# Two constant tiles of the causal mask product stored in bf16 instead of float32r

## The chip, the cores and the metric

One NeuronCore of one Trainium2 chip runs the whole program. The metric is the device time in microseconds (us). The kernel before takes 2742.83 us, the median of three runs (2741.75 to 2742.94).

## The reference

A decoder of two layers works on x, 4 batches of 512 rows with 256 features, and on a context of 4 x 1024 rows with 192 features. What is computed, in order:

```
x = LN(x + attn_L0(x))            # causal self-attention, 16 heads of 16
x = LN(x + xattn_L0(x, ctx))      # cross-attention, 1024 keys
x = LN(x + soft_moe_L0(x))        # 8 experts, 128 slots each
x = LN(x + attn_L1(x))            # causal self-attention
x = LN(x + xattn_L1(x, ctx))      # cross-attention
x = LN(x + block_L1(x))           # causal self-attention, then top-2 of 8 experts
```

In each causal layer the scores of query q against key k are `q.k/4`, with every k > q masked out, and then a softmax over k and the product with the values:

```
w = einsum('bhnd,bhmd->bhnm', q, k) / 4
w = where(tril, w, NEG); w = softmax(w); attn = einsum('bhnm,bhmd->bhnd', w, v)
```

## The kernel before, in words

There are three causal layers: a0 and a1, and a2 (the attention inside the last block). There are two cross layers, c0 and c1. `stage_attentions` runs twice: "first" does a0 and c0, "second" does a1, c1 and a2. Its work is cut into groups of four heads of one batch: 16 groups a layer, numbered n. `attention_plan` writes one list of events by hand (`body(n)`), and each engine walks it in order and does its own part. No planner with costs reorders it, apart from pieces of projections and norms that are spread in between by rough weights.

Heads have 16 features. Queries and keys are each split into two parts whose sum is the float32 value, so that one product with a contraction of 64 rows serves one head. Two heads (h = 0 and 1) lie in partitions 0 to 63 and 64 to 127, and are issued as a pair of products on the two halves of TensorE's rows; a second pair of heads is p = 0 or 1. These tiles are float32r (float32 read in one pass).

In a group, each head's scores are computed twice, in two layouts:

- `unit` (L1413): queries on partitions, keys along the columns. VectorE adds the mask and takes the row maximum (L1729 in causal layers; L1733 in cross layers, without a mask). A `chain` of small VectorE steps (L1757 to L1770) makes minus the maxima in bf16 parts, and TensorE turns them (L1467, `shift`, bf16) and ScalarE copies them out as `shift_T` (L1646, float32r).
- `scores`, event (t, p): the keys of key tile t (128 of them) on partitions, the queries from 128 t on along the columns: 512, 384, 256 and 128 columns for t = 0 to 3. Three kinds of product are added up in one PSUM bank for each h: the scores (L1426), in causal layers the mask (L1432), and the row maxima (L1436). ScalarE then takes the exponential (L1635).

`values` (L1448) multiplies the probabilities with the values, four heads side by side in 32 columns each (float32, 128 rows). All banks but one are shared by a ring of 7.

The code of a `scores` event on TensorE, from L1424 on:

```
for h in range(2):
    pe.matmul(bank_of(event, h)[:, q0:SEQ], keys_of(n)[own, p, ...], qs[r][own, p, q0:SEQ], start=True, stop=False)
if layer.causal:
    for x in range(2):
        for h in range(2):
            pe.matmul(bank_of(event, h)[:, q0:q0 + 64 * (x + 1)], c.pick[own, x, :],
                      c.mask_kq[own, x, 0:64 * (x + 1)], start=False, stop=False)
for h in range(2):
    filled(pe.matmul(bank_of(event, h)[:, q0:SEQ], c.choose[own, p, :], shift_T[n % 2][own, q0:SEQ], ...), event)
```

`pick` (the weights) holds two halves of an identity: half x picks rows 64 x to 64 x + 63 of the mask. `mask_kq` (the moving side) holds 0 or -1e30 for those 64 keys, and is used for 64 columns (x = 0) and 128 columns (x = 1). Each of the four mask products loads its own 128 columns of weights. There are 3 layers x 16 groups x 4 tiles x 2 = 384 causal `scores` events, and so 1536 mask products and as many weight loads.

Both tiles are made once, in `stage_constants`: GpSimd makes `ident_bf` and `tri_kq` in bf16, and VectorE copies them into `pick` and `mask_kq` (8 copies, L159).

Of the kernel before, what the change touches and what calls it, by code (L numbers as in the profile page):

```python
# [23 lines left out]
F32R = mybir.dt.float32r  # L24
BF16 = mybir.dt.bfloat16
# [5 lines left out]
P = 128  # L31
# [72 lines left out]
@staged  # L104
def stage_constants(c):

    nc = c.nc
    c.x_tok = c.keep("x_tok", [P, NT, D])  # L110
    c.ident = c.keep("ident", [P, P])
    c.ident_bf = c.keep("ident_bf", [P, P], BF16)
    c.pick = c.keep("pick", [P, 2, P], F32R)
    c.choose = c.keep("choose", [P, 2, P], F32R)
    c.mask_qk = c.keep("mask_qk", [P, SEQ])
    c.mask_kq = c.keep("mask_kq", [P, 2, P], F32R)
    c.eps = c.keep("eps", [P, 1])
    c.x_in = [c.ctx.enter_context(nc.semaphore(f"x_in{b}")) for b in range(BATCH)]
    c.made = c.ctx.enter_context(nc.semaphore("const_made"))
    filled = c.sem("const_filled")  # L120
    with (nc.sbuf_tensor("tri_kq", [P, P], BF16) as tri_kq,
          nc.sbuf_tensor("chosen", [P, 2, P], BF16) as chosen, nc.Block() as block):
        @block.sync
        def _(sp):
            for b in range(BATCH):
                sp.dma_start(c.x_tok[:, b * QT:(b + 1) * QT, :], c.args["x"][b].rearrange("(q p) d -> p q d", p=P)
                             ).then_inc(c.x_in[b], 16)

        @block.gpsimd
        def _(pool):  # L130
            for t in (c.ident, c.ident_bf, c.mask_qk, tri_kq):
                pool.memset(t[:, :], 0.0).then_inc(filled, 1)
            pool.memset(chosen[:, :, :], 0.0).then_inc(filled, 1)
            pool.memset(c.eps[:, :], LN_EPS).then_inc(c.made, 1)
            pool.wait_ge(filled, 5)
            for t in (c.ident, c.ident_bf):
                pool.affine_select(out=t[:, :], in_=t[:, :], compare_op=ALU.not_equal, fill=1.0, base=0,
                                   pattern=[[-1, P]], channel_multiplier=1).then_inc(c.made, 1)
            pool.affine_select(out=c.mask_qk[:, SEQ - P:SEQ], in_=c.mask_qk[:, SEQ - P:SEQ], compare_op=ALU.is_ge, fill=NEG_BIG,
                               base=0, pattern=[[-1, P]], channel_multiplier=1).then_inc(c.made, 1)  # L140
            pool.affine_select(out=tri_kq[:, :], in_=tri_kq[:, :], compare_op=ALU.is_ge, fill=NEG_BIG,
                               base=0, pattern=[[1, P]], channel_multiplier=-1).then_inc(c.made, 1)


            for i in range(6):
                if i:
                    pool.wait_ge(filled, 5 + 2 * i)
                for p in range(2):
                    pool.affine_select(out=chosen[:, p, :], in_=chosen[:, p, :], compare_op=ALU.not_equal, fill=1.0,
                                       base=-(64 * (i // 3) + 32 * p + i % 3), pattern=[[0, P]], channel_multiplier=1  # L150
                                       ).then_inc(filled, 1)

        @block.vector
        def _(v):
            v.wait_ge(c.made, 5)
            for dst, src in ((c.pick, c.ident_bf), (c.mask_kq, tri_kq)):
                for own in (slice(0, 64), slice(64, P)):
                    for x in range(2):
                        v.tensor_copy(dst[own, x, :], src[64 * x:64 * x + 64, :]).then_inc(c.made, 1)  # L159
            v.wait_ge(filled, 17)  # L160
            v.tensor_copy(c.choose[:, :, :], chosen[:, :, :]).then_inc(c.made, 1)
            v.wait_ge(c.made, CONSTANTS)
# [2359 lines left out]
def build(nc, args, out):  # L2522
    with ExitStack() as ctx:
        c = Core(nc, ctx, args, out)
        a = args
        stage_constants(c)

        def drams(name, keys):
# [170 lines left out]
```

## Time and profile before

| | us |
|---|---|
| median of three runs | 2742.83 |
| the profiled execution, own time | 2762.94 |
| its span, first to last instruction | 2761.2 |
| TensorE products busy in the span | 2504.2 (91%) |
| TensorE weight loads busy | 1439.7 (52%) |
| VectorE busy | 1496.9 (54%) |
| ScalarE busy | 1315.6 (48%) |

PE is TensorE's products and PEld its weight loads, which may overlap products. A busy time counts the latency of an instruction too, so that products in a pipeline overlap: their starts, not their lengths, show the pace. The mean granted clock of TensorE is 0.952 of full speed. The causal mask products run from 63 to 352 us (a0), 1345 to 1631 us (a1) and 2073 to 2332 us (a2); pieces of the layer after, and of the experts' gate in a2, lie among them.

### The profile page before, as it was taken

How to read it: one execution, taken by the hardware profiler on the slowest of the kernel's cores; microseconds unless marked ns; L12 is line 12 of the kernel's file. 1: busy time of each engine (PE TensorE's matmuls, PEld its weight loads, DVE VectorE, ACT ScalarE, POOL GpSimd, SP SyncE). 2: the span in 40 equal slices, each digit the busy share in tenths (PEclk: the TensorE clock that was granted, in tenths of full speed). 3: DMA queues.
4: the chain of work that ended last, by engine and by line, in shares of the span. 5: the costliest groups of instructions: out<-in, count | busy, mean ns of one | idle time of the engine just before them, and what ended most of it. 6: DMA issues, size and time to landing. Idle time of an engine off the chain costs nothing. (4 is left out here: it accounts for less than half of the span.)

```text
span 2761.2 us, 47077 instructions
## 1 busy us (share of the span) xinstructions
PE 2504.2 (91%) x15751; PEld 1439.7 (52%) x15752; DVE 1496.9 (54%) x4204; ACT 1315.6 (48%) x2826; POOL 455.4 (16%) x735
## 2 busy tenths in 40 slices
PE   5999999999979889999699999999998988599991
PEld 3555544444434456676365654444445555366761
DVE  2555777789744600013455598878756664322224
ACT  2655466677754521212255557766675543122220
POOL 4233212101100000000113322022122122110004
PEclk8999999999999999999799999999999987799995
DMA  7544534232800022203755443342322554121003
GB/s 222 160 142 142 144 100 107 54 85 58 267 1 1 1 98 67 95 12 115 201 151 142 140 115 85 81 107 62 109 77 81 165 165 148 52 63 34 31 31 97
DMA packets 156894, 276.76 MB, mean 100 GB/s; under 512 B 22928, under 2 KB 98960, under 8 KB 152208
## 3 DMA queue, kind: packets, MB, share of 16 engines
q1 hardware_dynamic: 152896, 262.56, 33.2%
q0 software_dynamic: 3792, 11.54, 1.3%
q8 instruction: 119, 1.95, 0.3%
q14 instruction: 87, 0.71, 0.1%
HBM read 195.51 MB, written 95.29 MB: 105 GB/s over the span
## 5 line engine op out<-in xcount | busy, mean ns | idle before, releaser
L1635 ACT ACTIVATE second_p<-psum 128x512 f32<-128x512 f32 (+3 forms) x1024 | 460.2, 524 | 248.7 <-PE psum L1436 233.4
L1635 ACT ACTIVATE first_p<-psum 128x512 f32<-128x512 f32 (+3 forms) x768 | 364.9, 551 | 150.1 <-PE psum L1436 146.8
L1733 DVE TENSOR_REDUCE second_max_parts<-psum 128x1 f32<-128x512 f32 x512 | 324.9, 685 | 54.6 <-PE psum L1413 44.5
L1733 DVE TENSOR_REDUCE first_max_parts<-psum 128x1 f32<-128x512 f32 x512 | 324.9, 685 | 52.0 <-PE psum L1413 42.7
L1729 DVE CUSTOM_DVE_ANT_0 second_masked<-psum,mask_qk 128x384 f32<-128x384 f32 (+3 forms) x512 | 229.7, 489 | 185.7 <-PE psum L1413 159.5
L1448 PE MATMUL psum<-second_p,second_v_aug 128*32 128x512 f32 (+3 forms) x2048 | 237.1, 535 | 0.5 <-ACT second_o_sum L1642 0.4
L1413 PE MATMUL psum<-second_k,second_q 64*128 64x512 f32 (+3 forms) x1024 | 211.9, 413 | 24.3 <-DMA second_k<-a_k_parts 11.4
L1426 PE MATMUL psum<-second_q,second_k 64*128 64x512 f32 (+3 forms) x1024 | 215.1, 416 | 5.8 <-DVE second_max_parts L1729 4.5
L1436 PE MATMUL psum<-second_shift_T,choose 64*128 64x512 f32 (+3 forms) x1024 | 198.3, 382 | 0.0
L1448 PE MATMUL psum<-first_p,first_v_aug 128*32 128x512 f32 (+3 forms) x1536 | 185.9, 556 | 1.2 <-ACT first_p L1635 0.7
L2512 ACT ACTIVATE routed_space<-psum,routed_bias 128x128 f32<-128x128 f32 x312 | 84.7, 382 | 213.3 <-PE psum L2437 213.3
L1729 DVE CUSTOM_DVE_ANT_0 first_masked<-psum,mask_qk 128x128 f32<-128x128 f32 (+3 forms) x256 | 114.5, 488 | 131.1 <-PE psum L1413 117.4
L1413 PEld LDWEIGHTS psum<-second_k,second_q 64*128 64x128 f32 x1024 | 101.2, 192 | 150.9 <-DVE second_max_parts L1733 87.1
L1413 PE MATMUL psum<-first_k,first_q 64*128 64x512 f32 (+3 forms) x768 | 166.0, 435 | 12.6 <-DMA first_k<-a_k_parts 6.6
L1426 PE MATMUL psum<-first_q,first_k 64*128 64x512 f32 (+3 forms) x768 | 163.0, 421 | 4.3 <-DVE first_max_parts L1733 3.4
L1426 PEld LDWEIGHTS psum<-second_q,second_k 64*128 64x128 f32 x1024 | 98.5, 188 | 113.0 <-issue 53.7
L1436 PE MATMUL psum<-first_shift_T,choose 64*128 64x512 f32 (+3 forms) x768 | 149.2, 384 | 0.0
L1413 PEld LDWEIGHTS psum<-first_k,first_q 64*128 64x128 f32 x768 | 74.1, 191 | 132.6 <-DVE first_max_parts L1733 85.5
L2427 PE MATMUL psum<-routed_up,routed_rows_T 128*128 x312 | 142.0, 598 | 0.9 <-issue 0.9
L2446 PE MATMUL psum<-routed_down,routed_space 128*128 x624 | 141.0, 379 | 0.0
L2134 DVE TENSOR_TENSOR soft_slots_T<-psum,soft_experts_down_bias 128x256 f32 (+1 forms) x32 | 13.6, 425 | 231.6 <-PE psum L2110 231.6
L1432 PEld LDWEIGHTS psum<-mask_kq,pick 64*128 64x128 f32 x1536 | 136.3, 193 | 4.6
(341 smaller groups left out, 3865.4 us busy)
## 6 DMA issues: line engine op xcount, KB each, us to landing
first_k<-c_k_parts SPq DMA_DIRECT2D x64, 256.0 KB, 4.7
second_q<-a_q_parts SPq DMA_DIRECT2D x128, 128.0 KB, 3.0
second_k<-a_k_parts SPq DMA_DIRECT2D x128, 128.0 KB, 3.0
second_k<-c_k_parts SPq DMA_DIRECT2D x64, 256.0 KB, 4.7
first_q<-a_q_parts SPq DMA_DIRECT2D x64, 128.0 KB, 3.2
first_k<-a_k_parts SPq DMA_DIRECT2D x64, 128.0 KB, 3.2
c_k_parts<-first_held SPq DMA_DIRECT2D x16, 512.0 KB, 3.1
first_q<-c_q_parts SPq DMA_DIRECT2D x64, 128.0 KB, 4.2
```

The lines of the kernel that those rows point to most:

```text
L1413: ins = pe.matmul(bank_of(event, h)[:, 0:width], qs[r][own, p, qt * P:(qt + 1) * P], keys_of(n)[own, p, k0:k0 + width], start=True, stop=True)
L1426: pe.matmul(bank_of(event, h)[:, q0:SEQ], keys_of(n)[own, p, t * P:(t + 1) * P], qs[r][own, p, q0:SEQ], start=True, stop=False)
L1432: pe.matmul(bank_of(event, h)[:, q0:q0 + 64 * (x + 1)], c.pick[own, x, :], c.mask_kq[own, x, 0:64 * (x + 1)], start=False, stop=False)
L1436: filled(pe.matmul(bank_of(event, h)[:, q0:SEQ], c.choose[own, p, :], shift_T[n % 2][own, q0:SEQ], start=False, stop=True), event)
L1448: ins = pe.matmul(c.psum[32 * j:32 * j + 32, PV_BANK, q0:SEQ], v_aug[n % 2][:, t, j, :], probs[at % 2][:, j, q0:SEQ], start=t == 0, stop=t ...
L1635: evacuated(act.activation(probs[tile % 2][:, 2 * h + p, q0:SEQ], bank[:, q0:SEQ], ACT.Exp, scale=scale), event)
L1729: evacuated(v.tensor_tensor_reduce(masked[:, done % 2, 0:width], bank[:, 0:width], c.mask_qk[:, SEQ - width:SEQ], 1.0, LEAST, ALU.add, ALU ...
L1733: evacuated(v.reduce_max(max_parts[n % 2][:, h, p, qt, k0 // BANK:k0 // BANK + 1], bank[:, 0:width], axis=AX_X), event)
L2134: v.tensor_tensor(eo[:, bass.ds(e, 1), t, :], c.psum[:, 4 + t, 0:D].unsqueeze(1), down_bias[r][:, :].unsqueeze(1), ALU.add).then_inc(s_rea ...
L2427: ins = pe.matmul(c.psum[:, UP_BANK + h, :], rows_T[r][:, k, :], up[:, bass.ds(e, 1), k, h * BANK:(h + 1) * BANK].rearrange("p o n -> p (o ...
L2446: ins = pe.matmul(c.psum[:, DOWN_BANK + r, 0:D], hidden[r][:, m, :], down[:, bass.ds(e, 1), m, :].rearrange("p o n -> p (o n)"), start=m = ...
L2512: act.activation(hidden[r][:, m, :], c.psum[:, TURN_BANK + m // PER, m % PER * P:(m % PER + 1) * P], ACT.Gelu, bias=bias[:, bass.ds(e * HM ...
```

## The change

Two tiles change their type, and nothing else in the program does. The products at L1432 then have bf16 on both sides. The products before and after them in the same bank (L1426, L1436) keep float32r. The copies at L159 become bf16 to bf16. The two tiles take 512 bytes of a partition each in place of 1024. The event lists are as before, in causal and in cross layers.

```diff
-    c.pick = c.keep("pick", [P, 2, P], F32R)
+    c.pick = c.keep("pick", [P, 2, P], BF16)
     c.choose = c.keep("choose", [P, 2, P], F32R)
     c.mask_qk = c.keep("mask_qk", [P, SEQ])
-    c.mask_kq = c.keep("mask_kq", [P, 2, P], F32R)
+    c.mask_kq = c.keep("mask_kq", [P, 2, P], BF16)
```

## Rows read from the trace of the kernel before

**Rows 1.** Busy time by engine in the three causal stretches.
```profile
core 0: us, PE busy (x) PEld busy (x) DVE busy (x) ACT busy (x) POOL busy (x), PEclk, DMA share, GB/s
63.00:352.00 289.00, 281.21 (x2278) 166.93 (x2276) 172.38 (x663) 159.87 (x369) 82.55 (x119) 0.98 0.52 147
1345.00:1631.00 286.00, 273.67 (x2248) 165.27 (x2244) 171.01 (x663) 154.48 (x358) 72.78 (x108) 0.97 0.54 147
2073.00:2332.00 259.00, 233.12 (x2088) 147.82 (x2084) 160.22 (x722) 125.58 (x312) 53.45 (x108) 0.89 0.42 129
```

**Rows 2.** Waits in 63 to 352 us: who waited for whom, total, times, longest.
```profile
DVE first_masked L1729 <- PE psum L1413: 76.9, 93, 2.6
ACT first_p L1635 <- PE psum L1436: 59.0, 58, 2.9
...
PEld psum L1426 <- DVE first_max_parts L1729: 13.5, 22, 0.8
```

**Rows 3.** The same in 2073 to 2332 us.
```profile
ACT second_p L1635 <- PE psum L1436: 92.4, 62, 4.6
...
PEld psum L1426 <- ACT second_p L1635: 13.2, 17, 1.8
...
PEld psum L1490 <- ACT second_oT L1650: 6.7, 2, 5.6
...
PEld psum L1426 <- DVE second_max_parts L1729: 5.9, 14, 0.8
```

**Rows 4.** Timeline, products then loads: a narrow event (t = 3) after a shift.
```profile
305.13 0.40 PE L1467 MATMUL psum<-ident_bf,first_shift 128*128 128x128 bf16 x4
305.46 0.33 PE L1426 MATMUL psum<-first_q,first_k 64*128 64x128 f32 x2
305.62 0.39 PE L1432 MATMUL psum<-mask_kq,pick 64*128 64x64 f32 x4
305.84 0.28 PE L1436 MATMUL psum<-first_shift_T,choose 64*128 64x128 f32 x2
305.95 0.45 PE L1413 MATMUL psum<-first_k,first_q 64*128 64x512 f32 x2
...
305.13 0.23 PEld L1467 LDWEIGHTS psum<-ident_bf,first_shift 128*128 128x128 bf16 x4 [0.41 <-issue]
305.45 0.19 PEld L1426 LDWEIGHTS psum<-first_q,first_k 64*128 64x128 f32 x2
305.56 0.30 PEld L1432 LDWEIGHTS psum<-mask_kq,pick 64*128 64x128 f32 x4
305.78 0.19 PEld L1436 LDWEIGHTS psum<-first_shift_T,choose 64*128 64x128 f32 x2
305.90 0.19 PEld L1413 LDWEIGHTS psum<-first_k,first_q 64*128 64x128 f32 x2
```

**Rows 5.** The same of a wide event (t = 0).
```profile
308.07 0.50 PE L1426 MATMUL psum<-first_q,first_k 64*128 64x512 f32 x2
308.42 0.33 PE L1432 MATMUL psum<-mask_kq,pick 64*128 64x64 f32 x4
308.59 0.45 PE L1436 MATMUL psum<-first_shift_T,choose 64*128 64x512 f32 x2
```

**Rows 6.** Loads of one form by line: busy us, mean ns of one.
```profile
L1432 PEld LDWEIGHTS psum<-mask_kq,pick 64*128 64x128 f32 x1536 | 136.3, 193 | 4.6
L1467 PEld LDWEIGHTS psum<-ident_bf,first_shift 128*128 128x128 bf16 x128 | 7.5, 99 | 14.9 <-issue 12.4 <-DVE first_shift L1770 2.6
```

**Rows 7.** Timeline of the loads: two bf16 loads before short products.
```profile
2215.35 0.10 PEld L1559 LDWEIGHTS psum<-second_both,second_tri 128*128 128x128 bf16 x1 [0.24 <-issue]
2215.36 0.10 PEld L1560 LDWEIGHTS psum<-second_earlier,second_ones 128*128 128x128 bf16 x1
```

**Rows 8.** Timeline of products: a change of tile shape, float32 on both sides.
```profile
237.70 0.22 PE L1413 MATMUL psum<-first_k,first_q 64*128 64x128 f32 x2
237.85 0.43 PE L1448 MATMUL psum<-first_p,first_v_aug 128*32 128x128 f32 x8
```

**Rows 9.** Timeline of the start: making the constants.
```profile
3.25 4.08 POOL L149 TENSOR_SCALAR_AFFINE_SELECT chosen<-chosen 128x128 bf16<-128x128 bf16 x12
3.32 1.05 DVE L159 CAST pick<-ident_bf 64x128 fp32r<-64x128 bf16 x4 [3.20 <-POOL tri_kq L141]
4.41 0.98 DVE L159 CAST mask_kq<-tri_kq 64x128 fp32r<-64x128 bf16 x4
7.37 0.29 DVE L161 CAST choose<-chosen 128x256 fp32r<-128x256 bf16 x1 [1.98 <-POOL chosen L149]
```

## The prediction

> **What bounds the kernel now.** I read the busy times of the three causal stretches first, since only they hold the changed products. In a0 the products are busy for 281 of 289 us and in a1 for 274 of 286, while VectorE and ScalarE stand at 54 to 60% [rows 1]. Busy time counts latency, so this alone does not prove that TensorE sets the pace. The waits do: in a0 VectorE waits 76.9 us for the products at L1413 and ScalarE 59.0 us for those at L1436, and the largest single wait of TensorE for another engine is 13.5 us [rows 2]. The other two engines are fed by TensorE. In a2 the balance is softer: 233 of 259 us, and TensorE waits 13.2 us for exponentials, 6.7 for a copy of outputs and 5.9 for maxima [rows 1, 3]. So time taken out of TensorE's stream counts nearly in full in a0 and a1, and less in a2.
>
> Then the timeline inside one `scores` event, to see whether products or weight loads set TensorE's pace. In the narrow event the loads start at 305.45, 305.56, (the second mask pair, inside the merged row of four), 305.78 and 305.90 [rows 4]: four steps over 0.45 us, 0.11 us for each pair of loads. The products between them have 128, 64, 128 and 128 columns. Had the columns set the pace, the pair with 64 would be followed twice as soon as those with 128; the step is the same for all. So here the loads are the limit, one pair each 0.11 us. A wide event shows the same behind its long first product: from the first mask product to the first of L1436 it is 308.59 - 308.42 = 0.17 us [rows 5]. I take a column at 0.42 ns, that is 2.4 GHz: the granted clock is 0.98 here, the upper of the two levels [rows 1]. The two mask pairs have 64 + 128 columns, 0.08 us; the rest is loading.
>
> **The loads.** The change halves nothing in the columns; what it can change is the load. A float32r load takes 193 ns in the mean, a bf16 load of the same 128 columns 99 ns [rows 6]. What counts is how soon the next may start. At L1559 and L1560 two bf16 loads start 0.01 us apart (2215.35 and 2215.36), before products of 32 columns [rows 7]; the four of L1467 fit in 0.23 us, three steps that hold (0.23 - 0.10)/3 = 0.04 us each with products of 128 columns between them [rows 4]. So a bf16 load holds the load path for 0.01 to 0.04 us where a float32r one holds it for 0.11. Both rows are loads of 128 rows; none in the trace has 64 rows in bf16, nor two halves side by side. I take 0.015, as the steps of L1467 are filled by products of 128 columns (0.053 us) anyway.
>
> The Trainium skill, page "TensorE: Matmul & The Clock Gate", section "LDWEIGHTS (loading the stationary operand)", puts a load at columns / 1.2 ns, 107 ns for 128, whatever the rows: the trace's step of 0.11 us agrees. The section "Weight-path perf modes" of the same page gives a faster load to 128 weights that are not FP32, four times in theory and about two times measured. By two times a bf16 load would hold the path for 54 ns and not for 15; that is my second case below.
>
> **The sum.** *Wide and middle events* (t = 0, 1, 2; 512, 384, 256 columns in the first product). The loads of the first mask pair lie behind the first product's columns and cost nothing now. The second mask pair's load must wait until the first mask pair has begun, and the load of L1436 until the second pair has: 0.11 us for the second. After the change the first mask pair's 64 columns (0.027 us) cover the 0.015 us of load. Gain 0.107 - 0.027 = 0.08 us. *Narrow events* (t = 3). Now it is 305.78 - 305.45 = 0.33 us from the first load to that of L1436 [rows 4]. After: the first load 0.107, its product's 128 columns 0.053, then the 64 columns 0.027 and the start of the second pair, in all 0.19. Gain 0.14 us. There are 96 events of each t: 96 x (3 x 0.08 + 0.14) = 36.5 us of TensorE's stream, 12.2 a layer.
>
> *What of it reaches the end.* Each place where TensorE waits for an engine that was not itself waiting for TensorE eats what was gained before it. Summing what TensorE's rows show against other engines, as in [rows 2, 3], I estimate 8% of a0's stretch, 11% of a1's and 19% of a2's in such waits, and their neighbourhood more: 0.85 of the gain in a0 and a1, 0.7 in a2. That is 12.2 x (0.85 + 0.85 + 0.7) = 29 us. What is late next is VectorE's masked maximum at L1729, and in a2 the exponential and the gate's chain.
>
> *The rest of the change.* The copies at L159 end near 5.4 us, and TensorE's start waits for `choose` at 7.37, which waits for GpSimd's 12 selects [rows 9]: faster or slower copies cost nothing up to 2 us. The moving side in bf16 gives nothing in columns, and its price cannot be less than the 0.027 us above. Half a kilobyte less of each tile only moves addresses: nothing.
>
> The profiled execution took 2762.94 us, 0.7% over the median of 2742.83. 29 us of the one are 29 us of the other: 2742.8 - 29 = 2714 us. As ends for the unknowns: 36.5 us all on the path and a little from a second-order effect (transfers and groups that begin earlier) gives 2702; loads at 54 ns give (3 x 0.054 + 0.107) x 96 = 26 us, and 0.6 of it 2727.
>
> **Rivals.** *A: the bf16 loads are faster, but two times.* 26 us of stream, 0.8 of it on the path: 2722 us. For it: no row has such loads with 64 rows, and a load lasts 99 against 193 ns, half [rows 6]. Against it: the starts 0.01 us apart [rows 7].
>
> *B: the gain is lost behind other engines.* The stream gets 36 us shorter, but VectorE and ScalarE come out as the bound, and less than 5 us are left: 2740. For it: a2's waits [rows 3]. Against it: 54 to 60% busy and waits of 1 us and more for TensorE in nearly each maximum [rows 1, 2].
>
> *C, slower: each change of type empties the array.* From L1426 to L1432 and from L1432 to L1436 the stream goes from float32r to bf16 and back. If such a change lets no load and no product in until the last has run out, it costs as much as the change of tile shape in the trace: 237.70 to 237.85 is 0.15 us for 128 columns of 0.053, so 0.096 us dead [rows 8]. 384 x 2 x 0.096 = 74 us against 36.5 saved, 37 on the stream and, at 0.8, about 30 us: 2773. It turns the sign from 0.048 us a change on. For it: no row has bf16 and float32r in one shape. Against it: leaving bf16 at L1467 for L1426 costs (305.46 - 305.31) - 0.053, again 0.10 us, where 305.31 is my estimate of the start of the fourth product: four products with 0.055 us between their starts (a column at 0.42 ns) from 305.13 on, rounded up by 0.015 for the first load [rows 4]; the shape changes there too, and type and shape together cost no more than shape alone.
>
> The Trainium skill, page "TensorEngine Tiling (Array Packing)", section "Key Properties", says that changing the tiling mode drains the engine, and changing the tile alone does not; it names no drain for a type. Rows 8 agree for the mode. By that rule the changed events, all of 64*128, have no drain.
>
> **Chances.** Forecast (loads well under 54 ns, most of it kept, 2703 to 2727): 0.67. A: 0.12. B: 0.08. C, or a smaller drain that still turns the sign: 0.13. 0.2%, 5.5 us, is about what a measurement of this kernel can tell from no change. Forecast and A are faster by more, 0.79; B is within, 0.08; C slower, 0.13. The range runs from 2702 (everything kept) to 2742, through A and B up to no change, and leaves C out.
>
> **What would show it.** Loads at L1432 of about 99 ns instead of 193; from the first mask product to L1436 0.09 us where it is 0.17, and 0.19 instead of 0.33 between the loads in a narrow event; the three stretches shorter by about 10, 10 and 9 us; VectorE's and ScalarE's waits for TensorE shorter, everything outside the causal layers as before. The forecast is wrong if the load step stays at 0.11 us, if a gap of some 0.1 us opens on either side of L1432, or if TensorE's waits at L1426 for VectorE and ScalarE grow by tens of us.

## The result, and the profile after

The changed kernel takes 2722.9 us (median of four, 2717.4 to 2723.6) against 2742.5 before; the ratio is 0.9924 with a 95% interval of 0.9907 to 0.9942. It is faster by about 20 us, where 29 were forecast.

The first profile of the kernel before stood 20 us over its unprofiled median, and most of that is in one place: a2 had a mean granted clock of 0.89 [rows 1]. A second profile of the same kernel (`before_again` below) has 0.94 there, a2 in 239.7 us instead of 259, and a span that fits the median. The comparison by stretches goes by it. First it, then the changed kernel; the stretches are a0, c0, a1, c1, a2 and the rest, with the columns of [rows 1].

```profile
core 0 of [0], span 2739.6 us
62.60:349.00 286.40, 278.59 (x2274) 165.26 (x2274) 171.94 (x662) 159.72 (x368) 82.09 (x119) 0.99 0.53 149
350.80:774.50 423.70, 411.30 (x2812) 188.85 (x2810) 331.55 (x652) 298.23 (x575) 67.36 (x128) 0.98 0.40 108
1341.60:1629.00 287.40, 273.68 (x2242) 165.13 (x2242) 170.59 (x662) 154.91 (x357) 72.29 (x108) 0.97 0.53 147
1630.80:2070.80 440.00, 428.33 (x2878) 197.18 (x2874) 342.80 (x704) 306.30 (x590) 84.04 (x137) 0.99 0.34 88
2072.70:2312.40 239.70, 222.96 (x2084) 141.49 (x2082) 160.25 (x722) 125.74 (x310) 53.31 (x108) 0.94 0.46 140
2312.40:2739.60 427.20, 330.45 (x1411) 229.52 (x1409) 130.94 (x321) 95.48 (x331) 61.42 (x69) 0.88 0.19 61
```

```profile
core 0 of [0], span 2721.8 us
62.20:343.90 281.70, 272.94 (x2272) 148.99 (x2272) 171.73 (x662) 157.65 (x368) 81.74 (x119) 0.98 0.54 151
345.80:767.60 421.80, 409.32 (x2810) 187.91 (x2808) 331.21 (x652) 298.09 (x575) 67.29 (x128) 0.99 0.41 109
1334.30:1615.60 281.30, 263.14 (x2242) 145.71 (x2242) 170.36 (x662) 152.33 (x357) 72.05 (x108) 0.98 0.55 150
1617.40:2058.40 441.00, 429.44 (x2876) 197.58 (x2872) 342.54 (x704) 306.31 (x590) 83.91 (x137) 0.99 0.34 88
2060.30:2293.20 232.90, 212.44 (x2086) 122.18 (x2082) 160.14 (x722) 123.46 (x311) 53.30 (x108) 0.95 0.49 144
2293.20:2721.80 428.60, 329.93 (x1411) 228.89 (x1407) 131.08 (x321) 95.17 (x331) 61.27 (x69) 0.88 0.19 61
```

The causal stretches give 4.7, 6.1 and 6.8 us, 17.6 of the 17.8 between the spans. The cross layers and the rest move by 1 to 2 us both ways; the change has nothing in them.

The 4.7 us of a0 are too few, because of the clock. Beside the low clock at its start, which both profiles have, two of its sixteen groups ran with a lower clock in the profile of the changed kernel, and none did in that of the kernel before. Here is the first of the two: in the kernel before, in the changed kernel, and in `same_bytes` (below), which has the same instructions as the changed kernel.

```profile
146.18:165.36 19.18, 17.73 (x152) 11.06 (x149) 11.32 (x45) 9.49 (x24) 3.24 (x3) 1.00 0.44 132
142.98:163.26 20.28, 18.75 (x153) 10.89 (x149) 11.19 (x45) 9.49 (x25) 3.23 (x3) 0.92 0.42 136
146.99:165.65 18.66, 17.13 (x153) 9.97 (x149) 11.20 (x45) 9.48 (x25) 3.23 (x3) 1.00 0.47 146
```

The group takes 20.28 us at a clock of 0.92 and 18.66 at 1.00. The other (211.97 to 232.27 us) takes 20.30 where the same kind of group takes 18.68. Without these 3.2 us a0 is shorter by 7.9 us. Over the whole program the clock is as good as the same (0.958 and 0.959).

All 1536 loads at L1432 are bf16 now. The view of that line gives the least, median and largest duration in ns:

```profile
L1432 PEld LDWEIGHTS psum<-mask_kq,pick x1536: 92/96/148, 62.8 to 2293.3; 64*128 64x128 bf16 x192
L1432 PE MATMUL psum<-mask_kq,pick x1536: 199/217/292, 62.8 to 2293.3; 64*128 64x64 bf16 x192
```

The timeline of a narrow event (t = 3), products and then loads, to be held against [rows 4]:

```profile
298.33 0.33 PE L1426 MATMUL psum<-first_q,first_k 64*128 64x128 f32 x2
298.49 0.26 PE L1432 MATMUL psum<-mask_kq,pick 64*128 64x64 bf16 x4
298.56 0.31 PE L1436 MATMUL psum<-first_shift_T,choose 64*128 64x128 f32 x2
...
298.32 0.19 PEld L1426 LDWEIGHTS psum<-first_q,first_k 64*128 64x128 f32 x2 [0.33 <-issue]
298.49 0.12 PEld L1432 LDWEIGHTS psum<-mask_kq,pick 64*128 64x128 bf16 x4
298.54 0.19 PEld L1436 LDWEIGHTS psum<-first_shift_T,choose 64*128 64x128 f32 x2
298.65 0.19 PEld L1413 LDWEIGHTS psum<-first_k,first_q 64*128 64x128 f32 x2
```

From the first load to the one after `choose` it is 298.65 - 298.32 = 0.33 us, where it was 305.90 - 305.45 = 0.45: a gain of 0.12. Two things are to be seen. The four bf16 loads take 0.12 us in all, and the load of L1436 follows the first of them by 0.05. But that first one starts 0.17 us after the event's first load, where the float32r one started after 0.11: it waits until the first product has streamed.

The wide event shows this more clearly. Loads before, then after:

```profile
308.07 0.19 PEld L1426 LDWEIGHTS psum<-first_q,first_k 64*128 64x128 f32 x2 [0.20 <-issue]
308.18 0.42 PEld L1432 LDWEIGHTS psum<-mask_kq,pick 64*128 64x128 f32 x4
308.53 0.19 PEld L1436 LDWEIGHTS psum<-first_shift_T,choose 64*128 64x128 f32 x2
```

```profile
300.74 0.19 PEld L1426 LDWEIGHTS psum<-first_q,first_k 64*128 64x128 f32 x2 [0.24 <-ACT first_shift_T L1646]
301.08 0.11 PEld L1432 LDWEIGHTS psum<-mask_kq,pick 64*128 64x128 bf16 x4 [0.16 <-issue]
301.13 0.19 PEld L1436 LDWEIGHTS psum<-first_shift_T,choose 64*128 64x128 f32 x2
```

The first mask load stands 0.11 us behind the first load before, and 0.34 after, when 512 columns have gone through. From the first load to that of L1436 it is 0.46 and 0.39 us: a gain of 0.07. By these two events the stream of TensorE is shorter by 96 x (3 x 0.07 + 0.12) = 32 us, against 36.5 in the prediction. They are typical: over the events at full clock whose loads follow one another without a break, some 210 of the 384, the medians of the same step are 0.067 us shorter for t = 0 and 1, 0.066 for t = 2 and 0.115 for t = 3, which makes 30 us.

The rest of the difference shows between groups. Each group has one set of four products of L1467, which the view merges into one row, so the distance of these rows is the length of a group. Four of a1, in the kernel before (second profile) and after:

```profile
1444.23 0.40 PE L1467 MATMUL psum<-ident_bf,second_shift 128*128 128x128 bf16 x4
1462.62 0.40 PE L1467 MATMUL psum<-ident_bf,second_shift 128*128 128x128 bf16 x4
1480.10 0.40 PE L1467 MATMUL psum<-ident_bf,second_shift 128*128 128x128 bf16 x4
1491.46 0.40 PE L1467 MATMUL psum<-ident_bf,second_shift 128*128 128x128 bf16 x4
```

```profile
1435.03 0.40 PE L1467 MATMUL psum<-ident_bf,second_shift 128*128 128x128 bf16 x4
1452.85 0.40 PE L1467 MATMUL psum<-ident_bf,second_shift 128*128 128x128 bf16 x4
1469.76 0.40 PE L1467 MATMUL psum<-ident_bf,second_shift 128*128 128x128 bf16 x4
1480.92 0.40 PE L1467 MATMUL psum<-ident_bf,second_shift 128*128 128x128 bf16 x4
```

The first distance is a *full* group, with pieces of projections between its events: 18.39 and 17.82 us, 0.57 less for its 8 events. The third is a *short* group with almost none: 11.36 and 11.16, 0.20 less for the same 8 events. By the medians above, the stream of 8 events is shorter by 0.63 us.

These two are the ends of a scale. All groups of a0 last over 15 us. Thirteen of its sixteen gain 0.44 to 0.57 us (the two with the lower clock by their lengths at full clock), the first 0.83, the last two 0.36 and 0.28. In a2 six groups are under 14 us, and they gain 0.12 to 0.33.

### The profile page after: what moved, and what is told of

It reads as the page before. It is cut to its first block and busy times, and to the rows that moved or that the text cites. A ratio compares the mean times of both kernels' runs of the same rounds, so it can differ in the third digit from the quotient of the medians.

```text
span 2721.8 us, 47077 instructions
## 1 busy us (share of the span) xinstructions
PE 2462.3 (90%) x15751; PEld 1374.4 (50%) x15752; DVE 1495.3 (55%) x4204; ACT 1308.7 (48%) x2826; POOL 454.0 (17%) x735
## 5 line engine op out<-in xcount | busy, mean ns | idle before, releaser
L1413 PE MATMUL psum<-second_k,second_q 64*128 64x512 f32 (+3 forms) x1024 | 211.5, 412 | 24.8 <-DMA second_k<-a_k_parts 14.2
L1426 PE MATMUL psum<-second_q,second_k 64*128 64x512 f32 (+3 forms) x1024 | 214.0, 414 | 7.8 <-DVE second_max_parts L1729 5.7
L1436 PE MATMUL psum<-second_shift_T,choose 64*128 64x512 f32 (+3 forms) x1024 | 205.5, 397 | 0.0
L1413 PE MATMUL psum<-first_k,first_q 64*128 64x512 f32 (+3 forms) x768 | 165.6, 434 | 13.9 <-DMA first_k<-a_k_parts 7.3
L1413 PEld LDWEIGHTS psum<-second_k,second_q 64*128 64x128 f32 x1024 | 100.6, 190 | 152.1 <-DVE second_max_parts L1733 87.9
L1426 PE MATMUL psum<-first_q,first_k 64*128 64x512 f32 (+3 forms) x768 | 162.8, 420 | 4.3 <-DVE first_max_parts L1733 3.5
L1426 PEld LDWEIGHTS psum<-second_q,second_k 64*128 64x128 f32 x1024 | 97.9, 187 | 114.8 <-issue 51.5
L1436 PE MATMUL psum<-first_shift_T,choose 64*128 64x512 f32 (+3 forms) x768 | 152.9, 394 | 0.0
L1413 PEld LDWEIGHTS psum<-first_k,first_q 64*128 64x128 f32 x768 | 73.6, 189 | 133.6 <-DVE first_max_parts L1733 86.9
L2446 PEld LDWEIGHTS psum<-routed_down,routed_space 128*128 128x128 f32 x624 | 115.6, 190 | 14.1
```

The lines of the kernel that those rows point to most:

```text
L1413: ins = pe.matmul(bank_of(event, h)[:, 0:width], qs[r][own, p, qt * P:(qt + 1) * P], keys_of(n)[own, p, k0:k0 + width], start=True, stop=True)
L1426: pe.matmul(bank_of(event, h)[:, q0:SEQ], keys_of(n)[own, p, t * P:(t + 1) * P], qs[r][own, p, q0:SEQ], start=True, stop=False)
L2446: ins = pe.matmul(c.psum[:, DOWN_BANK + r, 0:D], hidden[r][:, m, :], down[:, bass.ds(e, 1), m, :].rearrange("p o n -> p (o n)"), start=m = ...
```

## The experiments

The times are medians; the ratio is to the kernel before on the same chip. Its medians there were 2742.5 us for the change, 2742.3 for same_bytes, both twice runs and no_mask_f32r, 2742.0 for before_again, cols127 and choose_all, and 2743.4 (one run) for the two light runs. The last columns are the full and the short group of a1 by the distances of L1467, at the same two places of the plan as above.

| run | us | ratio, 95% interval | full group | short group |
|---|---|---|---|---|
| before_again | 2741.3 | one run | 18.39 | 11.36 |
| the change | 2722.9 | 0.9924 (0.9907 to 0.9942) | 17.82 | 11.16 |
| same_bytes | 2720.0 | 0.9914 (0.9894 to 0.9933) | 17.82 | 11.16 |
| twice_f32r | 2815.5 | 1.0262 (1.0242 to 1.0282) | 20.18 | 12.20 |
| twice_bf16 | 2740.7 | 0.9990 (0.9979 to 1.0001) | 18.42 | 11.42 |
| no_mask_f32r | 2688.3 | 0.9797 (0.9774 to 0.9821) | 16.82 | 10.68 |
| cols127 | 2723.8 | 0.9927 (0.9906 to 0.9949) | 17.94 | 11.20 |
| choose_all | 2705.5 | 0.9865 (0.9842 to 0.9889) | 17.37 | 10.95 |
| light_scalar | 2711.3 | one run | 17.77 | 10.42 |
| light_vector | 2707.0 | one run | 17.82 | 11.07 |

**same_bytes.**

```diff
-    c.pick = c.keep("pick", [P, 2, P], BF16)
+    c.pick = c.keep("pick", [P, 4, P], BF16)
-    c.mask_kq = c.keep("mask_kq", [P, 2, P], BF16)
+    c.mask_kq = c.keep("mask_kq", [P, 4, P], BF16)
```

> The changed kernel, with both bf16 tiles allocated twice as long, so that every other tile lies at the address it had before the change. Theory (the gain is the weight loads): as the changed kernel, 2723 us, within 0.2%. Rival (a few us of it come from shifted addresses): 2727 us or more, or under 2718 us.

2720.0 us, and both groups as in the changed kernel to 0.01 us. The addresses have no part in the gain.

**twice_f32r and twice_bf16.** The same edit, in the kernel before and in the changed one:

```diff
-                        for x in range(2):
+                        for x in (0, 1, 0, 1):
```

> The kernel before with the four mask products of each causal scores event issued twice (8 in place of 4; the masked scores get -2e30 in place of -1e30, which leaves the same probabilities). Theory (in float32r the load pace of 0.11 us a pair is what a mask product costs): two more pairs an event, 384 x 2 x 0.11 = 84 us of stream, nearly all on the path: about 2822 us. Rival (columns set the pace, 0.08 us an event): 31 us, 2773 us. If other engines already set much of the pace: under 60 us more.

> The changed kernel with its mask products issued twice in the same way. Theory (bf16 loads are hidden, so a pair costs its columns and some 0.01 us): 64 + 128 columns and two starts, about 0.10 us an event, 38 us of stream: about 2759 us. Rival (bf16 loads hold the path for half of a float32r load, 0.054 us): 0.12 to 0.13 us, 2770 us. The timeline tells these apart by the step between mask pairs: 0.03 and 0.06 us in the theory, no step under 0.054 in the rival.

A second set of float32r mask products costs 73 us (2815.5 - 2742.3), under the 80 of the theory and far over the rival's 31. In a full group it is 20.18 - 18.39 = 1.79 us, 0.22 an event: the two load steps of 0.11. A second set in bf16 costs 18 us (2740.7 - 2722.9), half of what I expected; in a full group 18.42 - 17.82 = 0.60, that is 0.075 us an event, about the 0.08 of the 64 + 128 columns alone. The steps between the loads of its four mask pairs say the same: 0.015, 0.030 and 0.057 us in the median, where the theory had 0.03 and 0.06 between sets and the rival nothing under 0.054. Starts of full groups, float32r and then bf16:

```profile
1476.22 0.40 PE L1467 MATMUL psum<-ident_bf,second_shift 128*128 128x128 bf16 x4
1496.40 0.40 PE L1467 MATMUL psum<-ident_bf,second_shift 128*128 128x128 bf16 x4
```

```profile
1443.67 0.40 PE L1467 MATMUL psum<-ident_bf,second_shift 128*128 128x128 bf16 x4
1462.09 0.40 PE L1467 MATMUL psum<-ident_bf,second_shift 128*128 128x128 bf16 x4
```

So a mask pair in bf16 is as cheap as its columns once bf16 products stand before it. The short groups show how little of it arrives there: 0.26 us for the second bf16 set, and 0.84 for the second float32r set.

**no_mask_f32r.**

```diff
-                    if layer.causal:
+                    if False:
```

(around the mask products only.)

> The kernel before without the mask products of the causal scores (left out of the computation; everything else in place). They take some 0.24 us of stream in a wide event and 0.22 in a narrow one, 90 us in all. Theory (about two thirds of what leaves TensorE's stream reaches the end, as in the change: 20 of 30 us): 60 us, 2682 us, with longer waits of TensorE for exponentials and maxima. Rival (nearly all of it reaches the end, and what the change lost went elsewhere, into a clock that falls more often or into gaps at L1432): 80 to 90 us, 2655 us.

2688.3 us, 54 less than before, of 90 expected on the stream. A full group loses 1.57 us (0.20 an event) of the 1.9 that the expectation puts on the stream of 8 events, a short one 0.68. So the loss between stream and end is largest in the short groups, with a smaller one in the full groups too, and it is not in the clock: the mean clock of the profiled run is 0.957, where the kernel before has 0.958 and the changed one 0.959. It also prices the first set in bf16: 17.82 - 16.82 = 1.00 us a full group, 0.125 an event, 0.05 more than the second set.

**before_again.** The file of the kernel before, unchanged.

> The kernel before once more, for a second profile. Its first one stood 20 us over the median of its unprofiled runs and had 55 us at half of the full clock in a2. Expected if that was chance: a span near 2741 us, 20 to 30 us at half clock in a2, and a2 near 243 us long; if the kernel before always has it under the profiler: again 259 us in a2.

A span of 2739.6 us and 239.7 in a2, as the first alternative has it. The 19 us more in the first profile came by chance, with a lower clock, and the profiler does not add 20 us.

**cols127.**

```diff
-  pe.matmul(bank_of(event, h)[:, q0:q0 + 64 * (x + 1)], c.pick[own, x, :],
+  pe.matmul(bank_of(event, h)[0:127, q0:q0 + 64 * (x + 1)], c.pick[own, x, 0:127],
```

> The changed kernel with mask products that load and write 127 of the 128 columns (the last key of each tile stays unmasked in this kernel). Theory (a bf16 load is fast only in the form of 128 columns in four strips): loads go back to one column a cycle or slower, at least 0.054 us a pair, and half or all of the gain is gone: 2730 to 2743 us, the steady group of a0 at 18.1 to 18.4 us. Rival (bf16 as such is fast): 2720 to 2723 us, 17.8 us.

Missed by the theory: 2723.8 us, and a full group of 17.94, only 0.12 over the changed kernel. Yet the load itself did change, to 137 ns in the mean from 97. A narrow event, loads:

```profile
299.99 0.19 PEld L1426 LDWEIGHTS psum<-first_q,first_k 64*128 64x128 f32 x2 [0.33 <-issue]
300.10 0.19 PEld L1432 LDWEIGHTS psum<-mask_kq,pick 64*127 64x127 bf16 x4
300.21 0.19 PEld L1436 LDWEIGHTS psum<-first_shift_T,choose 64*128 64x128 f32 x2
300.32 0.19 PEld L1413 LDWEIGHTS psum<-first_k,first_q 64*128 64x128 f32 x2
```

Two mask loads now take 0.11 us together (300.10 to 300.21), 0.055 each: half of a float32r load. And the first of them starts 0.11 us after the event's first load, as in float32r, ahead of the product that has yet to stream, where the load of 128 columns started after 0.17. The total from 299.99 to 300.32 is 0.33 us, as in the changed kernel. So bf16 itself gives most of the gain here: the slower form is started earlier, the faster form later, and the two come out 0.12 us a full group apart. The wait of the faster form is also not a matter of the type: the same bf16 on the same neighbours has none with 127 columns.

**choose_all.** The third product of an event goes the same way.

```diff
+    c.choose_bf = c.keep("choose_bf", [P, 2, P], BF16)
...
+    shift_B = [t[:, :].bitcast(BF16)[:, 0:SEQ] for t in shift_T]
...
-  filled(pe.matmul(..., c.choose[own, p, :], shift_T[n % 2][own, q0:SEQ], ...), event)
+  filled(pe.matmul(..., c.choose_bf[own, p, :], shift_B[n % 2][own, q0:SEQ], ...), event)
...
-  evacuated(act.activation(shift_T[event[1] % 2][:, :], bank, ACT.Copy), event)
+  evacuated(act.activation(shift_B[event[1] % 2][:, :], bank, ACT.Copy), event)
```

> The changed kernel with the third product of an event in bf16 as well: choose is bf16, and shift_T is written as bf16 (its values are bf16 parts already, so nothing is lost), in causal and cross layers. Theory: in a causal event the load of choose, 0.107 us behind the mask pair's 0.053 us of columns, goes out of the path, and the float32r load after it is hidden in a wide event: 0.05 to 0.08 us in each of 384 events, steady group of a0 at 17.2 to 17.4 us; in a cross event the load was hidden behind 512 columns and gains nothing, and may cost some 0.01 us as a bf16 load starts only when the float32r product has streamed: 5 us over 512 events. In all 2705 to 2712 us. Rival (a change between the types costs something that the mask pair hid): cross layers lose 0.03 us or more an event, and the sum is 2725 us or more.

2705.5 us (2702.1 to 2710.3), in the range of the theory and the best of the kernels here that compute everything: 37 us under the kernel before, 17 under the changed one. The full group goes to 17.37, 0.45 less, which is 0.056 us an event: the 0.05 that the first bf16 set cost beyond its columns. That was the load of `choose` in float32r, 0.11 us, of which the 128 columns before it hid half. The loads of a narrow event (the lines of this kernel stand 3 further down):

```profile
240.61 0.19 PEld L1429 LDWEIGHTS psum<-first_q,first_k 64*128 64x128 f32 x2
240.77 0.12 PEld L1435 LDWEIGHTS psum<-mask_kq,pick 64*128 64x128 bf16 x4
240.82 0.10 PEld L1439 LDWEIGHTS psum<-first_shift_T,choose_bf 64*128 64x128 bf16 x2
240.87 0.19 PEld L1416 LDWEIGHTS psum<-first_k,first_q 64*128 64x128 f32 x2
```

The load after `choose` follows it by 0.05 us instead of 0.11, and the event takes 0.26 us from its first load to there, where the changed kernel took 0.33. The cross layers show neither gain nor loss: their median group, by the distances of the same turning products, is 28.2 us in c0 and 29.1 in c1, as before.

**light_scalar and light_vector.** Who holds the short groups? (The groups of 11.4 and 11.6 us in these two expectations are counted from the first product of the scores.) The edit of light_scalar, then that of light_vector:

```diff
+  end = (q0 + SEQ) // 2 if layer.causal and n else SEQ
-  act.activation(probs[tile % 2][:, 2 * h + p, q0:SEQ], bank[:, q0:SEQ], ACT.Exp, scale=scale)
+  act.activation(probs[tile % 2][:, 2 * h + p, q0:end], bank[:, q0:end], ACT.Exp, scale=scale)
```

```diff
-    scale = 1.0 / float(HD) ** 0.5
+    scale = 0.0
-  v.tensor_tensor_reduce(masked[:, done % 2, 0:width], bank[:, 0:width], c.mask_qk[:, SEQ - width:SEQ], ...)
+  v.tensor_tensor_reduce(masked[:, done % 2, 0:width // 2], bank[:, 0:width // 2], c.mask_qk[:, SEQ - width // 2:SEQ], ...)
```

> The changed kernel with every exponential of a causal event but group 0's taken over half of its columns (the other half of the probabilities is left as it was). Question: in the groups of a1 that have almost no pieces of a projection, and last 11.4 us where they lasted 11.6 before the change, who holds the pace, as only 0.2 of the 0.5 to 0.6 us arrived? Theory (ScalarE's exponentials hold TensorE at L1426 through the shared banks): with light exponentials these groups fall to about 11.0 us, while the full groups stay at 17.8. Rival (VectorE's maxima hold it): 11.4 stays.

> The changed kernel with the masked maxima of a causal unit taken over half of its columns, and the exponential's scale at 0 so that nothing overflows (both change the result, the second changes no duration). Theory (ScalarE holds the short groups): 11.4 us stays. Rival (VectorE holds them): they fall to about 11.0 us. If both this run and the one with light exponentials shorten them a little, the two take turns; if neither does, it is TensorE's own stream, and the gain of a short group is small for another reason.

With light exponentials, then with light maxima (the third and fourth start, a short group):

```profile
1466.31 0.40 PE L1467 MATMUL psum<-ident_bf,second_shift 128*128 128x128 bf16 x4
1476.73 0.40 PE L1467 MATMUL psum<-ident_bf,second_shift 128*128 128x128 bf16 x4
```

```profile
1466.98 0.40 PE L1467 MATMUL psum<-ident_bf,second_shift 128*128 128x128 bf16 x4
1478.05 0.40 PE L1467 MATMUL psum<-ident_bf,second_shift 128*128 128x128 bf16 x4
```

10.42 and 11.07 us against 11.16; the full groups at the place of the table stay at 17.77 and 17.82. So this short group waits for ScalarE's exponentials above all, by up to 0.74 us, and a little for VectorE; this full one for neither.

Not every longer group is like it. Three groups of a0 go from 18.68 to 17.81 us with light exponentials, and one of a1 from 21.68 to 21.10 with light maxima. The totals, 2711.3 and 2707.0 us, are one run each and say little about which engine matters more: light_vector ran 214 us at half of the full clock, the changed kernel 226 and light_scalar 229.

## Why the prediction was right, and what was off in it

- *TensorE sets the pace in a0 and a1.* Right for the full groups of the table, shown by their indifference to lighter exponentials and maxima, and by 0.22 us a second float32r set, the whole load step. Not right for the short groups, where halved exponentials take off 0.74 us, and only in part for the three groups of a0 that lose 0.87.
- *The loads are the limit inside an event, 0.11 us a pair in float32r.* Right, by twice_f32r: 0.22 us an event, where the columns alone are 0.08.
- *A bf16 load holds the path for 0.015 us.* The figure holds between bf16 products: the second mask pair's load starts 0.015 us behind the first's in the median, and a second set costs 0.075 us, its columns. Taken for all of them it was too simple: the form of 128 columns does not start ahead of a running float32r product, so the first mask pair begins 0.01 to 0.02 us later than it could. The gain an event was mis-sized by this and by rounding: 0.07 and 0.12 us measured, 0.08 and 0.14 forecast, 30 to 32 us in place of 36.5. Rival A named the right price for the slower form (0.055 us a load in cols127) and, at 2722 us, came nearest to the measured time, but not by its mechanism: the kernel has the faster form, with later starts. The total alone can't tell the two apart (2722.9 and, with the slower form, 2723.8 us); the steps between loads do.
- *0.85 of the gain arrives in a0 and a1, 0.7 in a2.* Too high: 20 of some 31 us arrived, 0.65. This term and the one before it cost about the same, 4 to 5 us each, of the 9 by which the forecast was off. At equal clock a0 keeps 7.9 of 10 us, 0.79 where 0.85 was forecast. I had weighed the stretches by the share of time in which TensorE is seen to wait. What kind of group the events are in counts more: 0.57 us arrives in a full group and 0.20 in a short one, though TensorE is busy 11.0 of 11.4 us there too, as busy time includes latency. That the rest is lost to the exponentials is argued from light_scalar; float32r and bf16 were not compared with light exponentials in both.
- *The signs.* From the first mask product to L1436 it is 0.07 us (forecast 0.09), between the loads of a narrow event 0.21 (0.19). VectorE's wait for L1413 fell from 75.9 to 67.3 us in a0 and from 84.1 to 77.3 in a1. The waits that were to prove the forecast wrong by tens of us grew by a few. The largest growth at L1426, in a1, before and after:

```profile
PEld psum L1426 <- ACT second_p L1635: 5.3, 9, 0.7
PEld psum L1426 <- ACT second_p L1635: 8.7, 17, 1.0
```

- *Rival B, the gain is lost behind other engines.* Fell: 20 us are left and not under 5, though about a third of the gain does not arrive. One argument against it was misread: TensorE was not late for "nearly each maximum" by 1 us and more. VectorE waited before 93 of the 224 maxima in a0's stretch, 0.83 us each [rows 2].
- *Rival C, a drain at each change of type.* Fell: no gap opened, and the bf16 load of cols127 starts before the float32r product has streamed. The first mask product of the wide event starts 0.34 us behind the event's first product, as before (0.35), and L1436 follows it by 0.07, which is less than one drain of 0.096 alone would take. The Trainium skill, page "TensorEngine Tiling (Array Packing)", "Key Properties", names a drain for a change of tiling mode only. The trace agrees in that this change of type, in one tile shape, has none.
- The Trainium skill, page "TensorE: Matmul & The Clock Gate", "Weight-path perf modes", gives the fast load to 128 weights that are not FP32. The run with 127 columns agrees: 137 ns a load against 97. What it is worth here is 0.12 us of a full group of 18. The rest, 0.45, comes with bf16 in the slower form too: a load step of 0.055 us instead of 0.11, that is one cycle of 0.42 ns a column instead of two. Of the two factors that the prediction took from this section, the page gives "four times in theory" for fp8, not for bf16. "About two times" agrees with the durations here (191 against 97 ns) and not with the steps (0.11 against 0.015 us), and the steps decide.

Not settled: why the faster form waits for the running product. Whether it would also wait for one in bf16 that still has hundreds of columns to go was not tried.

## What to carry to other kernels

Where short products load their weights each time, look at whether the load and not the columns is their price. If it is, put both operands in bf16 where their values are exact there (a mask, an identity, a selector). Here that took the four mask products from 1.57 to 1.00 us of a full group. Look next at the load that follows, which becomes the exposed one. Read the step between starts, not the durations. And before scaling a saving by how busy the engine is, compare the kinds of groups in the stretch, and halve another engine's work in a trial kernel. The short groups that got shorter by it are those in which little of the saving arrived. It is a hint and no rule: the three groups of a0 that lost 0.87 us with light exponentials still kept 0.50 of the saving, as much as their neighbours.

## What the runs showed of the hardware that I had not expected

- A weight load of 128 columns in 64 rows holds the path for 0.11 us in float32r, 0.055 in bf16 with 127 columns, and 0.015 in bf16 with 128 (the median step in the changed kernel).
- The first two are started while the product before has yet to stream. The last is not, and stands 0.34 us behind the event's first load instead of 0.11 where that product has 512 columns of float32r. It costs almost nothing, since it is so short.
- Two profiles of one kernel differed by 21 us in span (2761.2 and 2739.6), with the granted clock in one stretch of 259 and 240 us at 0.89 and 0.94. Short falls within a stretch differ as well: one group of a0 took 20.28 us in one profile and 18.66 in another of the same instructions. A single profile with a clock below its fellows is no base for a stage's length.
